# Where softmax sums meet the attended values in the first attention phase: reciprocals turned beside them

## The chip, the cores and the metric

The kernel runs on one core of a Trainium2 chip. The metric is the device time of one execution in microseconds (us). TensorE (PE) multiplies and transposes, VectorE (DVE) and ScalarE (ACT) work elementwise, GpSimd (POOL) does some elementwise work, SyncE (SP) issues the DMAs.

## The reference, cut to what matters

Two layers of cross attention are applied to x of 16 batches x 256 tokens x 512 channels, with 16 heads of 32 channels. Only the first attention matters here:

```python
xq, ctx = layer_norm(x, qn_w, qn_b), layer_norm(context, cn_w, cn_b)
q = (xq @ q_w).reshape(B, N, H, D)
kv = (ctx @ kv_w).reshape(B, M, 2, H, D)
attn = jnp.einsum('bnhd,bmhd->bhnm', q, kv[:, :, 0]) * scale
attn = jnp.where(xa_mask[:, None, :, :], neg, attn)
attn = jax.nn.softmax(attn, axis=-1)
out = jnp.einsum('bhnm,bmhd->bnhd', attn, kv[:, :, 1]).reshape(B, N, C)
x = x + out @ proj_w + proj_b
```

An MLP, a causal self attention and another cross attention with its own MLP follow.

## The kernel before

The program has four phases, one after the other: mask (the attention above), mlp, causal, cross. The mask phase ends at about 722 us of the profiled span of 2908.9 us. Each phase but mlp runs one turn per batch; turns 1 to 14 are a hardware loop. In a turn every engine has its own queue of work, whose order is written out by hand in `mask_turn` (one for each engine), and engines wait for each other through counting semaphores. The turn of batch b also holds the start of batch b+1 (norms, turning to channels, the first queries, keys and values) and the end of batch b-1 (its last heads, the projection).

The 16 heads go in four quarters c of four heads; u counts the heads. For a quarter:

- PE `scores(b, c)` (L1529) makes the scores of four heads in four PSUM banks. It waits for the exponentials of the quarter before.
- DVE `minima` (L1086) adds the mask and takes the minimum of each row, four heads, two instructions a head, with `qk_lo` (L1045) in the middle.
- ACT `exps` (L650) takes the exponentials and leaves the sums of the rows in `sums`, an SBUF tile of 8 values a partition for each quarter (2 halves of the tokens x 4 heads).
- PE `turn_probs` (L1550) transposes them, ACT `copy` (L662) takes them to SBUF, PE `attend` (L1569) multiplies with the values. The quarter's result stands in the first half of the PSUM bank O, as 4 heads x 32 channels on the partitions and 256 tokens along them, and is not yet divided by the sums.
- ACT `attended` (L672) copies it to `OT`; PE `attended` (L1578) turns it to rows of tokens, 2 transposes into the second half of O; DVE `attended` takes the reciprocals of the 8 sums (L1094, tile `rs`) and multiplies (L1100) into `z`.
- For each half p of the channels, PE `post_turn` (L1587) turns z back to channels, 4 transposes into a PSUM bank; ACT `post_hi` (L685) rounds it to the high part of `zT`, DVE `post_lo` (L1150) makes the low part; PE `project` (L160, from `product`) multiplies with the projection matrix, and DVE `project` (L1160) adds it to the residual.

Two stretches of a turn matter below, with PE's order of work. Quarter 0 ends with queries, `post_turn`, keys. After `attend(b, 1)` PE goes on to

```python
                turn_probs(b, 8)
            if nxt:
                scores_taken(b, 10)
                turn_over(b + 1, 2)
                ...
                queries(b + 1, 0)
                scores_taken(b, 11)
                turn_over(b + 1, 3)
```

where `turn_over` (L1477) transposes the next batch's input into score banks that the exponentials must have left. ACT `turned` (L617) scales it, DVE `turned` (L1031, L1033) splits it into a high and a low part, and the next `keys(b + 1, 0, half)` (L160, from cT) wait for these, each half of the product for its own.

Of the kernel before, what the change touches and what calls it, by code (L numbers as in the profile page):

```python
# [13 lines left out]
ALU = mybir.AluOpType  # L14
ACT = mybir.ActivationFunctionType
AX_X = mybir.AxisListType.X

P = 128
# [145 lines left out]
def attention_phase(nc, kind, x_src, ctx_src, mask_src, dst, mats, vecs, common, last):  # L164
# [18 lines left out]
    if masked_ctx:  # L183
        x_in = rest("x_in", [P, TT, C])
        c_in = rest("c_in", [P, TT, C])
        xT = [rest(f"xT_{part}", [P, KC, S], F32R) for part in ("hi", "lo")]
        cT = [rest(f"cT_{part}", [P, KC, S], F32R) for part in ("hi", "lo")]
        QK = rest("qk_parts", [P, 2, 4, S], F32R)
        t32 = rest("t32", [P, 2, 2, S])
        r = room(4 * SLOT, SLOT)  # L190
        prob = r("prob", [P, 4, TT, S])
        V = r("v", [P, TT, H, DH])
        z = r("z", [P, TT, C])
        probT = room(5 * SLOT, SLOT)("probT", [P, 8, 512])
        r = room(6 * SLOT, SLOT)
        zT = [r(f"zT_{part}", [P, KC, S], F32R) for part in ("hi", "lo")]
        res = r("res", [P, TT, C])
        p_bias = r("p_bias", [P, C])
        OT = r("ot", [P, S])
        sums = r("sums", [P, KC, TT, HC])  # L200
        low = r("low", [P, 4, TT])
        rs = r("rs", [P, TT, HC])
        r = room(7 * SLOT, SLOT)
        stage = r("stage", [P, KC, C])
        mask = r("mask", [P, TT, S])
        m_in = r("m_in", [P, TT, S], U8)
        wcol = r("wcol", [P, 4, KC])
        stats = r("stats", [P, 4, 6])
        mv = r("mv", [P, 4, 2])
        minus_mean = r("minus_mean", [P, 4])  # L210
        rstd = r("rstd", [P, 4])
        raw = [probT[:, 0:4, :], probT[:, 4:8, :], prob[:].rearrange("p u t s -> p u (t s)"), stage[:]]
    else:
        xT = [rest(f"xT_{part}", [P, KC, S], F32R) for part in ("hi", "lo")]
        probT = rest("probT", [P, 8, 512])
        prob = rest("prob", [P, 4, TT, S])
        x_in = rest("x_in", [P, TT, C])
        z = rest("z", [P, TT, C])
        res = rest("res", [P, TT, C])
        r = room(3 * SLOT, SLOT)  # L220

        QK = r("qk_parts", [P, 2, 4, S], F32R)
        V = r("v", [P, TT, H, DH])
        OT = r("ot", [P, S])
        sums = r("sums", [P, KC, TT, HC])
        low = r("low", [P, 4, TT])
        rs = r("rs", [P, TT, HC])
        r = room(SLOT, SLOT)
        y = r("y", [P, TT, C])
        Q0 = r("q0", [P, 2, P], F32R)  # L230
        flags = r("flags", [P, S])
        cut = r("cut", [P, 2, S], F32R)
        lens = r("lens", [P, KC])
        nan0 = r("nan0", [P, KC])
        big = r("big", [P, TT])
        m_next = r("m_next", [P, TT])
        m_cur = r("m_cur", [P, TT])
        n_norms = 2 if cross else 1
        minus_mean = [r(f"minus_mean{i}", [P, TT]) for i in range(n_norms)]
        rstd = [r(f"rstd{i}", [P, TT]) for i in range(n_norms)]  # L240
        stats = r("stats", [P, TT, 6])
        mv = r("mv", [P, TT, 2])
# [358 lines left out]
    def scalar(act):  # L601
# [72 lines left out]

        def post_hi(b, p):

            act.wait_ge(s["post_ps"], 2 * (b - 1) + p + 1)
            if cross:

                for i in range(2):  # L680
                    ch = 2 * p + i
                    ins = act.activation(x2T[0][:, ch, :], POST_BANK[p][:, i * S:(i + 1) * S], ACT.Identity,  # L682
                                         scale=gb_col[:, 0, ch:ch + 1])
            else:
                ins = act.activation(zT[0][:, 2 * p:2 * p + 2, :],  # L685
                                     POST_BANK[p][:].rearrange("p (c t) -> p c t", c=2), ACT.Copy)
            ins.then_inc(s["post_hi"], 1)

        def relu(b, p):
# [300 lines left out]
        yield from turn(B, True, False, False)  # L990

    def vector(dve):
        head = {"mask": 7, "causal": 15, "cross": 14}[kind]
        per = {"mask": 6, "causal": 18, "cross": 23}[kind]
        chain = Chain(dve, s["chain"], head, per)
        def matrix_lo(i, quarters=range(KC)):
            for k in quarters:
# [74 lines left out]
        def masks_and_minima(b, u):  # L1072
# [14 lines left out]
                                                   ALU.min, low[:, u % 4, qt:qt + 1])  # L1087
            ins.then_inc(s["masked"], 1)

        def attended(b, c):  # L1090

            dve.wait_ge(s["z_ps"], KC * b + c + 1)
            c = c % KC
            chain.done(dve.reciprocal(rs[:], sums[:, c]))  # L1094
            chain.wait()
            if lengths:

                chain.done(dve.tensor_tensor(rs[:], rs[:], m_cur[:].unsqueeze(2).to_broadcast([P, TT, HC]), ALU.mult))
                chain.wait()
            dve.tensor_tensor(z[:, :, c * P:(c + 1) * P].rearrange("p t (h d) -> p t h d", h=HC),  # L1100
                              Oz, rs[:].unsqueeze(3).to_broadcast([P, TT, HC, DH]), ALU.mult
                              ).then_inc(s["z_done"], 1)
# [37 lines left out]
        def post_lo(b, p):  # L1140
            dve.wait_ge(s["post_hi"], 2 * (b - 1) + p + 1)
            if cross:
                for i in range(2):
                    ch = 2 * p + i
                    ins = dve.scalar_tensor_tensor(out=x2T[1][:, ch, :], in0=POST_BANK[p][:, i * S:(i + 1) * S],  # L1145
                                                   scalar=gb_col[:, 0, ch:ch + 1],
                                                   in1=x2T[0][:, ch, :].bitcast(F32), op0=ALU.mult,
                                                   op1=ALU.subtract)
            else:
                ins = dve.tensor_tensor(zT[1][:, 2 * p:2 * p + 2, :],  # L1150
                                        POST_BANK[p][:].rearrange("p (c t) -> p c t", c=2),
                                        zT[0][:, 2 * p:2 * p + 2, :].bitcast(F32), ALU.subtract)
            ins.then_inc(s["post_lo"], 1)

# [41 lines left out]

        def mask_turn(b, prev, cur, nxt):

            if cur:
                minima(b, 0, (0, 1))  # L1200
                qk_lo(b, 1)
                minima(b, 0, (2, 3))
            if not cur:
                yield ROOM
            if prev:
                attended(b, -1)
            if nxt:
                front(b + 1)
            elif cur:
# [2 lines left out]
                post_lo(b, 1)  # L1212

            if cur:
                minima(b, 1, (0, 1))
                qk_lo(b, 2)
                minima(b, 1, (2, 3))
                if not nxt:
                    yield ROOM
            if prev:  # L1220
                project(b, 0)
            if cur:
                attended(b, 0)
            if nxt:
                turned(b + 1, 0)
                turned(b + 1, 1)

            if cur:
                minima(b, 2, (0, 1))
                qk_lo(b, 3)  # L1230
                minima(b, 2, (2, 3))
# [5 lines left out]
            elif cur:  # L1237
                yield ROOM
            if cur:
                attended(b, 1)  # L1240

            if cur:
                minima(b, 3, (0, 1))
            if nxt:
                qk_lo(b + 1, 0)
# [4 lines left out]
            elif cur:  # L1250
                yield ROOM
            if cur:
                attended(b, 2)
                post_lo(b + 1, 0)
                if not nxt:
                    yield ROOM
# [206 lines left out]
    def tensor(pe):  # L1463
# [110 lines left out]
        def attended(b, c):  # L1574
# [3 lines left out]
                ins = pe.transpose(O[:, S + qt * P:S + (qt + 1) * P], OT[:, qt * P:(qt + 1) * P], ident[:])  # L1578
            ins.then_inc(s["z_ps"], 1)

        def post_turn(b, p):

            src = z if masked_ctx else res
            for i in range(2):
                for t in range(TT):
                    ch = 2 * p + i
# [50 lines left out]
        def mask_turn(b, prev, cur, nxt):  # L1637

            if cur:
                if prev:  # L1640
                    pe.wait_ge(s["post_lo"], 2 * (b - 1) + 1)
                scores(b, 0)
            if prev:
                turn_probs(b, -1)
# [4 lines left out]
            if not cur:  # L1649
                yield ROOM  # L1650
            if prev:
                attend(b, -1)
            if cur:
                values(b, 1, 1)
                turn_probs(b, 0)

            if prev:
                attended(b, -1)
            if cur:
                pe.wait_ge(s["qk_lo"], KC * b + 2)  # L1660
                queries(b, 2, 0)
                turn_probs(b, 1)
                queries(b, 2, 1)

            if prev:
                pe.wait_ge(s["z_done"], KC * b + 1)
                post_turn(b - 1, 1)
            if not cur:
                yield ROOM
            if cur:  # L1670
# [11 lines left out]
                project(b, 0, 0)  # L1682

            if cur:
                attend(b, 0)
            if prev:
                project(b, 0, 1)
# [1 line left out]
                turn_probs(b, 4)  # L1689

            if cur:
                attended(b, 0)
                pe.wait_ge(s["qk_lo"], KC * b + 3)
                queries(b, 3, 0)
                turn_probs(b, 5)
                queries(b, 3, 1)
# [19 lines left out]
                project(b, 1, 0)  # L1716

            if cur:
                attend(b, 1)
            if prev:  # L1720
                project(b, 1, 1)
# [14 lines left out]
            if cur:  # L1736
                turn_probs(b, 9)

            if cur:
                attended(b, 1)  # L1740
            if nxt:
                pe.wait_ge(s["t_lo"], NP * (b + 1) + 3)
                keys(b + 1, 0, 0)
# [17 lines left out]
                values(b + 1, 0, 0)  # L1761

            if cur:
                attend(b, 2)
            if nxt:
                values(b + 1, 0, 1)
            if cur:
                turn_probs(b, 12)

            if cur:  # L1770
                attended(b, 2)
            if nxt:
                pe.wait_ge(s["qk_lo"], KC * (b + 1) + 1)
                queries(b + 1, 1, 0)
# [1 line left out]
                turn_probs(b, 13)  # L1776
            if nxt:
                queries(b + 1, 1, 1)
            if cur:
                pe.wait_ge(s["z_done"], KC * b + 3)  # L1780
                scores_taken(b, 14)
                post_turn(b, 0)

            if nxt:
                keys(b + 1, 1, 0)
# [765 lines left out]
```

## Time and profile before

| | |
|---|---|
| median of 3 runs | 2909.57 us (2909.24 to 2912.53) |
| profiled execution, its time and its span | 2911.72 us, 2908.9 us |
| busy share of the span: PE, PE weight loads | 96%, 84% |
| DVE, ACT, POOL | 60%, 56%, 22% |
| mean granted TensorE clock | 0.985 |

Shares are over all four phases; the mask phase is about a quarter of the span. An instruction's length in the trace overlaps the next one's, so what a piece of work costs an engine is read from start to start.

### The profile page before, as it was taken

The page shows a single profiled execution, that of the slowest core. Times are in us where ns is not written, and L with a number is a line of the kernel's source. Part 1 is how long each engine was busy: PE and PEld are TensorE (multiplying, and loading weights), DVE is VectorE, ACT ScalarE, POOL GpSimd, SP SyncE. Part 2 cuts the span into 40 slices and gives each one's busy share as a digit, 9 for nine tenths or more (in the row PEclk, how much of TensorE's full clock was granted, in tenths as well). Part 3 has the DMA queues.
Part 4 walks back from the last instruction along what each step waited for, and adds up shares of the span by engine and source line. Part 5 has one row for each costly group of instructions (what it writes and reads, how often), then busy time and mean ns, then how long its engine had stood idle before and what let it go on. Part 6 is the DMA issues. An engine that isn't in the chain of part 4 may idle for free. (4 is left out here: it accounts for less than half of the span.)

```text
span 2908.9 us, 69038 instructions
## 1 busy us (share of the span) xinstructions
PE 2800.9 (96%) x24864; PEld 2434.5 (84%) x24864; DVE 1747.2 (60%) x5353; ACT 1634.4 (56%) x4947; POOL 625.4 (22%) x760
## 2 busy tenths in 40 slices
PE   7999999998999999999999999997899999999995
PEld 6888888887788888888889999996788888888884
DVE  5666666666433333333367777776576767777674
ACT  6777777777311111111277777776575666666562
POOL 1111110111000000000013333333132434333243
PEclk9999999999999999999999999998899999999997
DMA  3111111112300000001001111113201111111100
GB/s 115 31 59 59 38 51 59 51 38 77 109 29 29 19 9 29 29 29 65 22 27 59 46 43 43 43 43 106 73 31 44 42 43 43 43 36 36 43 29 22
DMA packets 74804, 134.37 MB, mean 46 GB/s; under 512 B 10096, under 2 KB 10096, under 8 KB 74736
## 3 DMA queue, kind: packets, MB, share of 16 engines
q1 hardware_dynamic: 74736, 133.47, 13.7%
q8 instruction: 42, 0.69, 0.1%
q14 instruction: 26, 0.21, 0.0%
HBM read 99.90 MB, written 33.55 MB: 46 GB/s over the span
## 5 line engine op out<-in xcount | busy, mean ns | idle before, releaser
L2263 ACT ACTIVATE mlp_h<-mlp_f,mlp_b1col 128x512 f32<-128x512 f32 x128 | 88.2, 689 | 548.2 <-PE mlp_f L2406 548.2
L2406 PE MATMUL mlp_f<-mlp_xT_hi,mlp_w 128*128 128x512 f32 x1024 | 336.5, 391 | 5.2 <-PEq L91 5.2
L2334 DVE CAST mlp_hT_hi<-mlp_h 128x512 fp32r<-128x512 f32 x128 | 58.4, 457 | 434.7 <-ACT mlp_h L2263 434.7
L2418 PE MATMUL mlp_acc<-mlp_w,mlp_hT_hi 128*128 128x512 f32 x1024 | 316.9, 391 | 1.0 <-DVE mlp_hT_lo L2336 1.0
L650 ACT ACTIVATE cross_prob<-cross_scores,cross_low 128x256 f32<-128x256 f32 x512 | 237.4, 499 | 14.5 <-DVE cross_low L1080 14.5
L650 ACT ACTIVATE mask_prob<-mask_scores,mask_low 128x256 f32<-128x256 f32 x512 | 236.9, 474 | 11.5 <-DVE mask_low L1086 10.9
L1086 DVE CUSTOM_DVE_ANT_0 mask_scores<-mask_scores,mask_mask 128x256 f32<-128x256 f32 x512 | 201.3, 455 | 62.9 <-PE mask_scores L1529 62.4
L2406 PEld LDWEIGHTS mlp_f<-mlp_xT_hi,mlp_w 128*128 128x128 f32 x1024 | 193.0, 188 | 45.6 <-issue 5.6
L160 PE MATMUL causal_work<-causal_xT_hi,causal_w 128*128 128x256 f32 x1008 | 226.6, 296 | 0.0
L2418 PEld LDWEIGHTS mlp_acc<-mlp_w,mlp_hT_hi 128*128 128x128 f32 x1024 | 191.1, 188 | 40.3 <-DVE mlp_hT_lo L2336 1.4
L650 ACT ACTIVATE causal_prob<-causal_scores,causal_low 128x128 f32<-128x128 f32 (+1 forms) x512 | 211.1, 433 | 21.7 <-DVE causal_low L1086 20.5
L2406 PE MATMUL mlp_f<-mlp_xT_lo,mlp_w 128*128 128x512 f32 x512 | 199.8, 390 | 0.0
L2418 PE MATMUL mlp_acc<-mlp_w,mlp_hT_lo 128*128 128x512 f32 x512 | 199.5, 390 | 0.0
L1086 DVE CUSTOM_DVE_ANT_0 causal_scores<-causal_scores,causal_tri 128x128 f32<-128x128 f32 (+1 forms) x512 | 164.3, 392 | 33.0 <-PE causal_scores L1535 33.0
L160 PEld LDWEIGHTS causal_work<-causal_xT_hi,causal_w 128*128 128x128 f32 x1008 | 169.4, 189 | 12.1 <-issue 12.1
L1080 DVE TENSOR_REDUCE cross_low<-cross_scores 128x2 f32<-128x512 f32 x256 | 159.8, 680 | 14.2 <-PE cross_scores L1535 10.7
L488 POOL TENSOR_SCALAR cross_q<-all_own_head,cross_qk_parts 128x128 fp32r<-128x128 f32 x128 | 59.8, 478 | 421.2 <-DVE cross_qk_parts L1045 411.5
L160 PE MATMUL causal_work<-causal_xT_lo,causal_w 128*128 128x256 f32 x504 | 141.9, 282 | 0.0
L488 POOL TENSOR_SCALAR causal_q<-all_own_head,causal_qk_parts 128x128 fp32r<-128x128 f32 x128 | 57.7, 462 | 389.1 <-DVE causal_qk_parts L1045 381.9
L457 POOL TENSOR_TENSOR mask_rstd<-mask_rstd,all_half 128x4 f32<-128x4 f32 x16 | 16.3, 1019 | 538.8 <-DVE mask_rstd L1017 538.8
L662 ACT ACTIVATE cross_probT<-cross_probsT 128x512 f32<-128x512 f32 x128 | 76.4, 597 | 98.9 <-PE cross_probsT L1550 98.9
L160 PE MATMUL mask_work<-mask_cT_hi,mask_w 128*128 128x256 f32 x504 | 120.8, 303 | 3.8 <-DVE mask_cT_lo L1033 1.5
(276 smaller groups left out, 8275.5 us busy)
## 6 DMA issues: line engine op xcount, KB each, us to landing
mask_x_in<-in_x SPq DMA_DIRECT2D x16, 512.0 KB, 3.7
mask_c_in<-in_ctx SPq DMA_DIRECT2D x16, 512.0 KB, 5.2
mask_res<-in_x SPq DMA_DIRECT2D x16, 512.0 KB, 3.6
after_attention<-mask_res SPq DMA_DIRECT2D x16, 512.0 KB, 5.9
mlp_x<-after_attention SPq DMA_DIRECT2D x8, 1024.0 KB, 5.7
mlp_stage<-in_L_xattn_fc_w SPq DMA_DIRECT2D x8, 1024.0 KB, 5.2
after_layer<-mlp_y SPq DMA_DIRECT2D x8, 1024.0 KB, 4.3
causal_x_in<-after_layer SPq DMA_DIRECT2D x16, 512.0 KB, 4.2
```

What stands on the lines that cost most here:

```text
L160: last = pe.matmul(out, lhs(k, a), rhs(k, c), start=(k == 0 and n == 0), stop=(k == KC - 1 and n == len(PASSES) - 1))
L457: pool.tensor_tensor(rstd[:], rstd[:], common.half[:], ALU.pow).then_inc(s["rstd_ready"], 1)
L488: ins = pool.tensor_scalar(Q0[:, part, :], own_head[:], QK[:, c % 2, 1 - part, 0:1].bitcast(F32), 1.0, ALU.mult, ALU.mult)
L650: ins = act.activation(prob[:, u % 4, qt, 0:w], SC[h][:, FROM[qt]:FROM[qt] + w], ACT.Exp, bias=low[:, u % 4, qt:qt + 1], scale=-1.0, accum ...
L662: act.activation(probT[:, u % 8, 0:n], PT_BANK[u % HC][:, 0:n], ACT.Copy).then_inc(s["copied"], 1)
L1080: ins = dve.tensor_reduce(low[:, u % 4, :], SC[h][:].rearrange("p (t k) -> p t k", t=TT), AX_X, ALU.min)
L1086: ins = dve.tensor_tensor_reduce(SC[h][:, at], SC[h][:, at], extra, 1.0, F32_MAX, ALU.add, ALU.min, low[:, u % 4, qt:qt + 1])
L2263: act.activation(h32[:, m % 2, :], F1[m % 2][:], ACT.Gelu, bias=b1col[:, m:m + 1]).then_inc(s["gelu"], 1)
L2334: dve.tensor_copy(hT[0][:, r, :], h32[:, r, :]).then_inc(s["h_hi"], 1)
L2406: ins = pe.matmul(F1[m % 2][:], W[2 * (m // 4)][:, a, k, m % 4 * P:(m % 4 + 1) * P], xT[p][:, k, :], start=(k == 0 and n == 0), stop=(k == ...
L2418: ins = pe.matmul(ACC[t][:], hT[a][:, m % 2, t * P:(t + 1) * P], W[2 * (m // 4) + 1][:, p, m % 4, :], start=(m == 0 and n == 0), stop=(m = ...
```

## The change

DVE takes the reciprocals with each of the 8 sums repeated over the 32 channels of its head, so that `rs` has 256 values a partition in place of 8 (`over_sums`). It stands at the head of each quarter's minima in DVE's queue. PE turns `rs` into the second half of O right ahead of `attend` (`turn_sums`, 2 transposes), in the place of turning OT. DVE multiplies OT with it (`normed`), channels on the partitions, into `z32`, which `post_hi` and `post_lo` read from SBUF. `post_turn` is gone from the mask phase, and so are the waits around it. The other phases keep their way. The core of the diff:

```diff
-        z = r("z", [P, TT, C])
+        z32 = r("z32", [P, KC, S])
-        rs = r("rs", [P, TT, HC])
+        rs = r("rs", [P, TT, HC, DH])
...
+                act.wait_ge(s["z_done"], KC * (b - 1) + 2 * p + 3)
+                if p == 0 and (not isinstance(b, int) or b > 1):
+                    act.wait_ge(s["proj_ps"], TT * (b - 1))
+                ins = act.activation(zT[0][:, 2 * p:2 * p + 2, :], z32[:, 2 * p:2 * p + 2, :], ACT.Copy)
...
+        def over_sums(b, c):
+            dve.wait_ge(s["exp_done"], UNITS * b + HC * (c + 1))
+            dve.reciprocal(rs[:], sums[:, c % KC].unsqueeze(3).to_broadcast([P, TT, HC, DH])).then_inc(s["rs_done"], 1)
+        def normed(b, c):
+            dve.wait_ge(s["ot_done"], KC * b + c + 1)
+            dve.tensor_tensor(z32[:, c % KC, :], OT[:], O[:, S:2 * S], ALU.mult).then_inc(s["z_done"], 1)
...
             if cur:
+                over_sums(b, 1)
                 minima(b, 2, (0, 1))
                 qk_lo(b, 3)
                 minima(b, 2, (2, 3))
...
+        def turn_sums(b, c):
+            pe.wait_ge(s["rs_done"], KC * b + c + 1)
+            pe.wait_ge(s["z_done"], KC * b + c + 1)
+            for qt in range(TT):
+                pe.transpose(O[:, S + qt * P:S + (qt + 1) * P], rs[:, qt].rearrange("p h d -> p (h d)"), ident[:])
...
             if cur:
-                if prev:
-                    pe.wait_ge(s["post_lo"], 2 * (b - 1) + 1)
                 scores(b, 0)
...
             if prev:
+                turn_sums(b, -1)
                 attend(b, -1)
...
-            if prev:
-                attended(b, -1)
...
-            if prev:
-                pe.wait_ge(s["z_done"], KC * b + 1)
-                post_turn(b - 1, 1)
...
-            if cur:
-                pe.wait_ge(s["z_done"], KC * b + 3)
-                scores_taken(b, 14)
-                post_turn(b, 0)
```

In the same way `over_sums(b, c - 1)` stands ahead of `minima(b, c, ...)` for every quarter, `turn_sums(b, c)` ahead of every `attend(b, c)`, and `normed(b, c)` where DVE's `attended(b, c)` stood. `sums` and `low` move to another place in SBUF.

## Rows read from the trace of the kernel before

**Rows 1.** Windows: each engine's busy us (and instructions), granted TensorE clock, DMA share, GB/s.

```profile
300.00:400.00 100.00, 99.55 (x977) 84.91 (x976) 65.71 (x237) 78.39 (x238) 18.07 (x20) 1.00 0.13 43
```

**Rows 2.** Groups of 60 to 700 us: names, shapes, count; busy us, mean ns; idle before, releaser.

```profile
L160 PEld LDWEIGHTS mask_work<-mask_cT_hi,mask_w 128*128 128x128 f32 x480 | 82.3, 189 | 10.7 <-DVE mask_cT_lo L1033 10.7
...
L1100 DVE TENSOR_TENSOR mask_z<-mask_attended,mask_rs 128x256 f32<-128x256 f32 x60 | 25.5, 424 | 2.1
...
L1587 PE MATMUL mask_attended<-all_ident,mask_z 128*128 128x128 f32 x60 | 9.0, 273 | 0.0
```

**Rows 3.** Timeline of PE, quarter 0: start us, length us, line, output, input, count.

```profile
381.74 0.28 PE L160 MATMUL mask_work<-mask_xT_hi,mask_w 128*128 128x256 f32 x1
381.86 0.60 PE L1587 MATMUL mask_attended<-all_ident,mask_z 128*128 128x128 f32 x4
382.22 0.37 PE L160 MATMUL mask_work<-mask_cT_hi,mask_w 128*128 128x256 f32 x1
382.42 0.28 PE L160 MATMUL mask_work<-mask_cT_lo,mask_w 128*128 128x256 f32 x1
```

**Rows 4.** Timeline of PE, quarters 1 and 2 of the same turn.

```profile
395.00 0.98 PE L1529 MATMUL mask_scores<-mask_qk_parts 32*128 32x256 f32 x24
...
397.89 1.07 PE L1569 MATMUL mask_attended<-mask_probT,mask_v 128*32 128x256 f32 x16
...
400.82 0.60 PE L1477 MATMUL mask_scores<-all_ident,mask_c_in 128*128 128x128 f32 x4
...
404.03 0.39 PE L160 MATMUL mask_work<-mask_cT_hi,mask_w 128*128 128x256 f32 x1
...
405.59 0.39 PE L160 MATMUL mask_work<-mask_cT_hi,mask_w 128*128 128x256 f32 x1
```

**Rows 5.** Timeline of DVE in quarters 1 and 2; the bracket is idle time and its releaser.

```profile
385.44 0.43 DVE L1086 CUSTOM_DVE_ANT_0 mask_scores<-mask_scores,mask_mask 128x256 f32<-128x256 f32 x1 [0.81 <-PE mask_scores L1529]
...
395.47 0.69 DVE L1033 TENSOR_TENSOR mask_xT_lo<-mask_t,mask_xT_hi 128x512 fp32r<-128x512 f32 x1
396.19 0.43 DVE L1086 CUSTOM_DVE_ANT_0 mask_scores<-mask_scores,mask_mask 128x256 f32<-128x256 f32 x1
...
402.82 0.43 DVE L1031 CAST mask_cT_hi<-mask_t 128x512 fp32r<-128x512 f32 x1 [1.55 <-ACT mask_t L617]
...
404.38 0.43 DVE L1031 CAST mask_cT_hi<-mask_t 128x512 fp32r<-128x512 f32 x1 [0.41 <-ACT mask_t L617]
```

**Rows 6.** Timeline of ACT in quarters 1 and 2.

```profile
391.66 0.60 ACT L662 ACTIVATE mask_probT<-mask_scores 128x512 f32<-128x512 f32 x1 [0.53 <-PE mask_scores L1550]
392.89 1.93 ACT L617 ACTIVATE mask_t<-mask_scores,mask_wcol 128x256 f32<-128x256 f32 x4 [0.64 <-PE mask_scores L1477]
...
397.10 0.47 ACT L650 ACTIVATE mask_prob<-mask_scores,mask_low 128x256 f32<-128x256 f32 x1
...
401.26 0.62 ACT L662 ACTIVATE mask_probT<-mask_scores 128x512 f32<-128x512 f32 x1
401.74 1.05 ACT L617 ACTIVATE mask_t<-mask_scores,mask_wcol 128x256 f32<-128x256 f32 x2
403.33 1.02 ACT L617 ACTIVATE mask_t<-mask_scores,mask_wcol 128x256 f32<-128x256 f32 x2 [0.54 <-PE mask_scores L1477]
```

**Rows 7.** Short DVE instructions, from their tile: count, ns min/median/max, first and last start.

```profile
L1094 DVE RECIPROCAL causal_rs<-causal_sums x64: 192/202/206, 1474.3 to 2024.8; 128x8 f32<-128x8 f32 x64
L1098 DVE TENSOR_TENSOR causal_rs<-causal_rs,causal_m_cur x64: 166/167/246, 1474.5 to 2025.1; 128x8 f32<-128x8 f32 x64
...
L1058 DVE RECIPROCAL causal_nan<-causal_lens x64: 149/155/158, 1453.0 to 2006.5; 128x1 f32<-128x1 f32 x64
L1060 DVE TENSOR_SCALAR causal_nan<-causal_nan x64: 152/154/156, 1453.2 to 2006.7; 128x1 f32<-128x1 f32 x64
```

**Rows 8.** Timeline of PE at the end of the mask phase.

```profile
717.39 1.60 PE L1569 MATMUL mask_attended<-mask_probT,mask_v 128*32 128x256 f32 x16
...
721.10 0.47 PE L2406 MATMUL mlp_f<-mlp_xT_hi,mlp_w 128*128 128x512 f32 x1
```

More of the change, by code:

```diff
@@ L199, in attention_phase @@
         OT = r("ot", [P, S])
-        sums = r("sums", [P, KC, TT, HC])
-        low = r("low", [P, 4, TT])
-        rs = r("rs", [P, TT, HC])
+        rs = r("rs", [P, TT, HC, DH])
         r = room(7 * SLOT, SLOT)
@@ L207, in attention_phase @@
         wcol = r("wcol", [P, 4, KC])
+        sums = r("sums", [P, KC, TT, HC])
+        low = r("low", [P, 4, TT])
         stats = r("stats", [P, 4, 6])
@@ L675, in post_hi @@
         def post_hi(b, p):
-            act.wait_ge(s["post_ps"], 2 * (b - 1) + p + 1)
             if cross:
+                act.wait_ge(s["post_ps"], 2 * (b - 1) + p + 1)
                 for i in range(2):
@@ L684, in post_hi @@
             else:
-                ins = act.activation(zT[0][:, 2 * p:2 * p + 2, :],
-                                     POST_BANK[p][:].rearrange("p (c t) -> p c t", c=2), ACT.Copy)
+                act.wait_ge(s["z_done"], KC * (b - 1) + 2 * p + 3)
+                if p == 0 and (not isinstance(b, int) or b > 1):
+                    act.wait_ge(s["proj_ps"], TT * (b - 1))
+                ins = act.activation(zT[0][:, 2 * p:2 * p + 2, :], z32[:, 2 * p:2 * p + 2, :], ACT.Copy)
             ins.then_inc(s["post_hi"], 1)
@@ L992, in vector @@
     def vector(dve):
-        head = {"mask": 7, "causal": 15, "cross": 14}[kind]
-        per = {"mask": 6, "causal": 18, "cross": 23}[kind]
+        head = {"mask": 4, "causal": 15, "cross": 14}[kind]
+        per = {"mask": 2, "causal": 18, "cross": 23}[kind]
         chain = Chain(dve, s["chain"], head, per)
@@ L1095, in attended @@
             chain.wait()
-            if lengths:
-                chain.done(dve.tensor_tensor(rs[:], rs[:], m_cur[:].unsqueeze(2).to_broadcast([P, TT, HC]), ALU.mult))
-                chain.wait()
+            chain.done(dve.tensor_tensor(rs[:], rs[:], m_cur[:].unsqueeze(2).to_broadcast([P, TT, HC]), ALU.mult))
+            chain.wait()
             dve.tensor_tensor(z[:, :, c * P:(c + 1) * P].rearrange("p t (h d) -> p t h d", h=HC),
@@ L1149, in post_lo @@
             else:
-                ins = dve.tensor_tensor(zT[1][:, 2 * p:2 * p + 2, :],
-                                        POST_BANK[p][:].rearrange("p (c t) -> p c t", c=2),
+                ins = dve.tensor_tensor(zT[1][:, 2 * p:2 * p + 2, :], z32[:, 2 * p:2 * p + 2, :],
                                         zT[0][:, 2 * p:2 * p + 2, :].bitcast(F32), ALU.subtract)
@@ L1197, in mask_turn @@
         def mask_turn(b, prev, cur, nxt):
+            if prev:
+                over_sums(b, -1)
             if cur:
@@ L1205, in mask_turn @@
             if prev:
-                attended(b, -1)
+                normed(b, -1)
             if nxt:
@@ L1214, in mask_turn @@
             if cur:
+                over_sums(b, 0)
                 minima(b, 1, (0, 1))
@@ L1222, in mask_turn @@
             if cur:
-                attended(b, 0)
+                normed(b, 0)
             if nxt:
@@ L1239, in mask_turn @@
             if cur:
-                attended(b, 1)
+                normed(b, 1)
             if cur:
+                over_sums(b, 2)
                 minima(b, 3, (0, 1))
@@ L1252, in mask_turn @@
             if cur:
-                attended(b, 2)
+                normed(b, 2)
                 post_lo(b + 1, 0)
@@ L1579, in attended @@
             ins.then_inc(s["z_ps"], 1)
+        def turn_sums(b, c):
[3 more added lines that the diff above has]
+                pe.transpose(O[:, S + qt * P:S + (qt + 1) * P], rs[:, qt].rearrange("p h d -> p (h d)"), ident[:])
         def post_turn(b, p):
-            src = z if masked_ctx else res
+            src = res
             for i in range(2):
@@ L1655, in mask_turn @@
                 turn_probs(b, 0)
-            if prev:
-                attended(b, -1)
             if cur:
@@ L1684, in mask_turn @@
             if cur:
+                turn_sums(b, 0)
                 attend(b, 0)
@@ L1691, in mask_turn @@
             if cur:
-                attended(b, 0)
                 pe.wait_ge(s["qk_lo"], KC * b + 3)
@@ L1718, in mask_turn @@
             if cur:
+                turn_sums(b, 1)
                 attend(b, 1)
@@ L1737, in mask_turn @@
                 turn_probs(b, 9)
-            if cur:
-                attended(b, 1)
             if nxt:
@@ L1763, in mask_turn @@
             if cur:
+                turn_sums(b, 2)
                 attend(b, 2)
@@ L1768, in mask_turn @@
                 turn_probs(b, 12)
-            if cur:
-                attended(b, 2)
             if nxt:
@@ L1778, in mask_turn @@
                 queries(b + 1, 1, 1)
-            if cur:
-                pe.wait_ge(s["z_done"], KC * b + 3)
-                scores_taken(b, 14)
-                post_turn(b, 0)
             if nxt:
```

## Prediction

> **What bounds the kernel now.** I read the windows first: in a hundred microseconds of the mask phase PE is busy for 99.55, at the full granted clock of 1.00, while ACT has 78.39 and DVE 65.71 [rows 1]. So PE's queue sets the pace, and the reader could think that any transpose taken from it is a gain. The groups then show where PE is not its own master: from 60 to 700 us its weight loads sat idle for 10.7 us until DVE had written the low part of cT, and the z that this change is about costs DVE 60 multiplications of 424 ns and PE 60 transposes for each of two banks, of which one is shown [rows 2]. That idle time is small, but it lies in every turn at one place, the keys of the next batch. The timelines of PE, DVE and ACT there show a closed ring [rows 4 to 6]: PE starts `scores(b, 2)` at 395.00; DVE, which ends `turned(b+1, 1)` (its last instruction starts at 395.47), starts the minima at 396.19; ACT starts the exponentials of quarter 2 at 397.10, runs them without a pause worth the name, then `copy(b, 8)` at 401.26 and `turned(b+1, 2)` at 401.74; DVE casts at 402.82; PE starts the first half of the keys at 404.03 and the second at 405.59. In this ring PE waits; elsewhere in the turn it does not. A turn is thus a stretch in which PE sets the time, from the keys round to `turn_over(b+1, 0)`, and the ring of some 10 us, where DVE and ACT set it.
>
> **What PE gains.** A `post_turn` stands between queries and keys. From the last matmul of the queries to the second of the keys is 382.42 - 381.74 = 0.68 us; two plain steps there take 2 x 0.12 (381.86 - 381.74), so the four transposes cost PE 0.44, 0.11 each [rows 3]. Batches have two; 30 of them lie where PE sets the pace (two in each of 15 turns), which gives 30 x 0.44 = 13.2 us. The one of batch 15 ahead of the last turn is beside waits for exponentials and counts nothing. The two transposes of OT become two of rs in each quarter: 0.22 off, 0.22 on, and nothing is summed; they move ahead of `attend`, and if the step between different weight shapes cost another 0.1 us there, 64 of them would be 6 us, a bound that I keep for the range.
>
> At the end of the phase PE waits for OT, turns it, waits for z and turns that: `attend` starts at 717.39 and its 1.60 us end at 718.99, and the mlp's first matmul starts at 721.10 [rows 8]. With only ACT's copy and one multiplication left, both beside that mlp work, PE goes straight on. I take 2.0 of these 2.1 us. Together 15.2 us.
>
> **What DVE pays.** The reciprocal over 256 values is in no row. One value takes 155 ns, where a plain instruction takes 154; eight take 202, where a plain one of the same shape takes 167 [rows 7]. So eight reciprocals cost 35 ns over a plain instruction, 4.4 ns each. A plain one over 256 is 424 ns [rows 2]. That gives 0.424 + 256 x 0.0044 = 1.55 us, which I take, since the fixed part falls out between equal shapes. The floor is the plain 0.42. From one value to eight the medians differ by 47 ns, 6.7 ns a value, so 0.155 + 255 x 0.0067 = 1.87; with the longest of eight and the shortest of one (206 - 149) it is 8.1 ns and 2.22 us, the ceiling.
>
> The Trainium skill bears on this: "VectorE: DVE Perf Modes", in "First, the fixed hardware budget", says that the reciprocal is an iterative divide with a repeat count of 8. Read as eight steps for each value, and with the spacing of the plain rows, it would be near the ceiling and not near the value taken, and it speaks against widening a reciprocal from 8 values to 256. The trace's 35 ns for eight values agree only in that a value costs several plain steps.
>
> The small reciprocal and its wait go (0.2 us a quarter); DVE waits for ACT's OT and not for PE's turn of it, so `normed` comes about 1 us earlier in most quarters. DVE thus has room for four wide reciprocals a turn; what matters is what stands behind each.
>
> - Quarters 3 and 0 of a turn (`over_sums(b, 2)` and `over_sums(b, -1)`): DVE idles before the minima for longer than the instruction takes, or comes free about as `scores` ends. Nothing at 1.55, some tenths at 2.22.
> - Quarter 1 (`over_sums(b, 0)`): DVE idled for 0.81 us before the minima at 385.44 [rows 5]; it also gains about 1 us from the earlier `normed`. The minima come up to 0.3 us late. ACT behind them waits for PE for 0.53 us and again for 0.64 before `turned(b+1, 0)` [rows 6], and swallows 1.17. Cost nothing; without that cover it would be up to 0.3 us a turn.
> - Quarter 2 (`over_sums(b, 1)`): no cover. The instruction can start when the step before gives way, 395.47 + 0.60 = 396.07 (such a 0.69 us instruction is followed after about 0.60), and holds the next for its length less 0.08. The minima start at 396.07 + 1.47 = 397.54 in place of 396.19: 1.35 us late. Queued behind it are the minima, `qk_lo(b, 3)`, DVE's `project(b, 1)` and the turned parts. ACT has no gap up to `turned(b+1, 2)`, so the cast and the first keys are 1.35 late. The second half of the keys follows the first by 1.56 us now, of which about 0.36 is a wait for `turned(b+1, 3)` that then goes, since ACT no longer waits its 0.54 us for PE [rows 4, 6]. PE's turn grows by 1.35 - 0.36 = 0.99 us.
>
> PE also meets two new waits: `turn_sums(b, 1)` needs rs at about 397.6, ahead of an `attend` now at 397.89, so it is just ready; and the step to `turn_over(b+1, 2)`, now 400.82, waits for later exponentials. Both lie inside the 0.99 and are not added. 15 turns have a next batch: 15 x 0.99 = 14.9 us. `post_hi` and `post_lo` work on the same 512 columns from SBUF; they end earlier, not later, since they don't wait for PE, and nobody waits for them.
>
> **The sum.** Against the profiled execution: 2911.7 - 15.2 + 14.9 = 2911.4 us. It stood 2.1 us above the median of the runs, so I predict 2909 us.
>
> **Rivals.** I call no change what lies within 0.2%, about what a measurement of this kernel tells from none: 2903.8 to 2915.4.
>
> 1. The two cancel, as above. Chance 0.48. It holds for a reciprocal of about 1.2 to 2.0 us; own range 2904 to 2915.
> 2. The lateness doesn't bite: the reciprocal is at the floor (0.42 us, minima 0.22 late, less than the 0.36), or the ring has more give than I see. Then 15.2 us are kept: 2894 us. For: PE is busy for 99.55 of 100 us, and its transposes are surely gone. Against: eight reciprocals already take 35 ns too long, and the trace shows DVE as PE's releaser in this ring. It decides below 1.2 us. Halfway, at 0.8 us, it gives 15 x (0.60 - 0.36) = 3.6 us of loss and 2898. Chance 0.29.
> 3. The wide reciprocal is as slow as the ceiling. The minima of quarter 2 are then 2.02 us late and a turn pays 1.66: 15 x 1.66 = 24.9, less 15.2, that is 9.7 us more: 2919 us. It is slower from 2.0 us of reciprocal on. For: 8.1 ns can be read from the extremes, and `over_sums` of quarters 0 and 1 would begin to show (0.3 us a turn is 4 us more, 2923). Against: medians give 4.4 to 6.7. The skill's repeat count in the same section as above, taken at its word, is this case. Chance 0.23.
>
> So faster 0.29, same 0.48, slower 0.23. The two tails beyond 2897 and 2921 hold about a tenth each: the range is 2897 to 2921.
>
> **What would show it.** The reciprocal of 128x256: 1.5 us in case 1, 0.4 in case 2, 2.2 in case 3. DVE's minima of quarter 2 start 1.35 us later after `scores(b, 2)` than the 1.19 us now. PE's group of L1587 has no mask rows left. PE's idle time released by DVE's cT parts or by ACT's exponentials grows from 0.7 to about 1.7 us a turn, in the ring and nowhere else. The mlp's first matmul follows the last `attend` at once. I would be wrong if PE waited for rs in other quarters, if a pair of transposes ahead of `attend` cost more than 0.22 us, or if ACT's chain after the late minima caught up.

## The result and the profile after

The changed kernel takes 2914.39 us (median of 22 runs, 2911.64 to 2919.03) where the kernel before takes 2910.19 (22 runs). The ratio is 1.0014, interval [1.0008, 1.0020]: slower by some 4 us, less than the 0.2% that I had called a difference, but beyond the interval and not the way of the 2909 that I forecast. All ratios here and below compare executions at the usual mean clock of 0.98 or 0.99; one of seven executions of the first experiment's kernel took 3907 us at a mean granted clock of 0.653 and is not in its ratio.

The windows of the profile after, the same stretch as in [rows 1]:

```profile
300.00:400.00 100.00, 97.48 (x959) 82.64 (x958) 76.17 (x230) 77.02 (x233) 17.94 (x18) 1.00 0.14 43
```

PE, which was busy for 99.55, is now at 97.48, at the same clock of 1.00; DVE went from 65.71 to 76.17. PE has less to do and stands idle for more than what it was spared. The waits of 60 to 700 us (who waited for whom: us in total, times, longest) say where:

```profile
PEld mask_work L160 <- DVE mask_cT_lo L1036: 13.7, 14, 1.0
PEld mask_scores L1492 <- issue: 10.5, 14, 0.8
...
PE mask_work L160 <- DVE mask_cT_lo L1036: 10.4, 14, 0.7
...
PE mask_scores L1492 <- ACT mask_prob L650: 7.3, 14, 0.5
...
PEld mask_attended L1601 <- DVE mask_rs L1096: 4.8, 14, 0.4
```

PE waits once a turn for the low part of cT, once for the exponentials to leave the score banks (L1492 is `turn_over`), and shortly for rs. All three lie in the ring. The weight loads' rows (PEld) add up to (13.7 + 10.5 + 4.8) / 14 = 2.1 us a turn, where the kernel before had the 10.7 us of [rows 2], 0.8 a turn; I had expected 0.7 to become 1.7. PE's timeline there, the turn that answers to [rows 4]:

```profile
394.75 0.98 PE L1544 MATMUL mask_scores<-mask_qk_parts 32*128 32x256 f32 x24
...
397.62 0.44 PE L1601 MATMUL mask_attended<-all_ident,mask_rs 128*128 128x128 f32 x2
397.99 1.07 PE L1584 MATMUL mask_attended<-mask_probT,mask_v 128*32 128x256 f32 x16
...
401.60 0.65 PE L1492 MATMUL mask_scores<-all_ident,mask_c_in 128*128 128x128 f32 x4 [0.52 <-ACT mask_prob L650]
...
405.30 0.38 PE L160 MATMUL mask_work<-mask_cT_hi,mask_w 128*128 128x256 f32 x1 [0.74 <-DVE mask_cT_lo L1036]
...
407.35 0.98 PE L1544 MATMUL mask_scores<-mask_qk_parts 32*128 32x256 f32 x24
```

From the scores of quarter 2 to those of quarter 3 PE takes 407.35 - 394.75 = 12.60 us. In the kernel before the first of these start at 395.00 [rows 4] and the second, in the same timeline, here:

```profile
406.49 0.98 PE L1529 MATMUL mask_scores<-mask_qk_parts 32*128 32x256 f32 x24
```

That is 11.49, so the ring grew by 1.11 us. A whole turn (from a quarter 0 to the next) went from 42.98 to 43.22 us, so the rest of it shrank by 0.87. DVE and ACT in the ring, answering to [rows 5, 6]:

```profile
395.21 0.69 DVE L1036 TENSOR_TENSOR mask_xT_lo<-mask_t,mask_xT_hi 128x512 fp32r<-128x512 f32 x1
395.82 1.75 DVE L1096 RECIPROCAL mask_rs<-mask_sums 128x256 f32<-128x256 f32 x1
397.48 0.41 DVE L1089 CUSTOM_DVE_ANT_0 mask_scores<-mask_scores,mask_mask 128x256 f32<-128x256 f32 x1
```

```profile
396.35 0.60 ACT L662 ACTIVATE mask_probT<-mask_probsT 128x512 f32<-128x512 f32 x1 [0.81 <-PE mask_probsT L1565]
398.37 0.47 ACT L650 ACTIVATE mask_prob<-mask_scores,mask_low 128x256 f32<-128x256 f32 x1 [1.42 <-DVE mask_low L1089]
```

The minima start 2.73 us after the scores of their quarter (397.48 - 394.75), 1.19 before: 1.54 late. ACT, which had no gap, waits 1.42 us for them. The instruction in between is the term that I had to guess; its tile's rows give all 64 (ns min/median/max):

```profile
L1096 DVE RECIPROCAL mask_rs<-mask_sums x64: 1735/1746/1749, 39.1 to 718.8; 128x256 f32<-128x256 f32 x64
```

1.746 us, where I took 1.55. At the end of the phase the last `attend` is at once followed by the mlp, as forecast, but PE had stood 1.43 us for rs in the last turn, which answers to [rows 8]:

```profile
709.56 0.44 PE L1601 MATMUL mask_attended<-all_ident,mask_rs 128*128 128x128 f32 x2 [1.43 <-DVE mask_rs L1096]
...
721.06 1.07 PE L1584 MATMUL mask_attended<-mask_probT,mask_v 128*32 128x256 f32 x16
722.06 0.50 PE L2416 MATMUL mlp_f<-mlp_xT_hi,mlp_w 128*128 128x512 f32 x1
```

### The profile page after: what moved, and what is told of

Its sections match the earlier page's. It is cut to its first block and busy times, and to the rows that moved or that the text cites. A ratio compares the mean times of both kernels' runs of the same rounds, so it can differ in the third digit from the quotient of the medians.

```text
span 2911.2 us, 68814 instructions
## 1 busy us (share of the span) xinstructions
PE 2789.9 (96%) x24736; PEld 2419.3 (83%) x24736; DVE 1834.4 (63%) x5353; ACT 1637.6 (56%) x4947; POOL 632.9 (22%) x760
## 5 line engine op out<-in xcount | busy, mean ns | idle before, releaser
L650 ACT ACTIVATE cross_prob<-cross_scores,cross_low 128x256 f32<-128x256 f32 x512 | 237.8, 500 | 12.8 <-DVE cross_low L1083 12.7
L1083 DVE TENSOR_REDUCE cross_low<-cross_scores 128x2 f32<-128x512 f32 x256 | 159.8, 680 | 13.6 <-PE cross_scores L1550 10.2
L662 ACT ACTIVATE mask_probT<-mask_probsT 128x512 f32<-128x512 f32 x128 | 76.9, 601 | 93.9 <-PE mask_probsT L1565 93.9
```

Of the source, the lines that this page charges most:

```text
L650: ins = act.activation(prob[:, u % 4, qt, 0:w], SC[h][:, FROM[qt]:FROM[qt] + w], ACT.Exp, bias=low[:, u % 4, qt:qt + 1], scale=-1.0, accum ...
L662: act.activation(probT[:, u % 8, 0:n], PT_BANK[u % HC][:, 0:n], ACT.Copy).then_inc(s["copied"], 1)
L1083: ins = dve.tensor_reduce(low[:, u % 4, :], SC[h][:].rearrange("p (t k) -> p t k", t=TT), AX_X, ALU.min)
```

## The experiments

Theory A: the wide reciprocal ahead of quarter 2's minima lengthens the ring, and only that costs. Theory B: PE's wait for rs costs. Theory C: the added work on DVE costs wherever it stands. Each change below is made to the changed kernel unless said otherwise; "turn" is read from the starts of the scores of one quarter in two turns. Ratios are to the kernel before, run beside each on the same chip (2910.53 to 2911.91 us there); the changed kernel was not run again beside them, and the kernel before alone stood up to 1.7 us higher there than beside it, so a difference to its 2914.39 us is good to about 2 us.

**The same work, earlier in the queue**

```diff
                 normed(b, 0)
+                over_sums(b, 1)
             if nxt:
                 turned(b + 1, 0)
                 turned(b + 1, 1)
             if cur:
-                over_sums(b, 1)
                 minima(b, 2, (0, 1))
```

> The changed kernel with one move: quarter 1's over_sums stands right behind normed(b, 0), ahead of turned(b+1, 0), where VectorE idles, and no longer ahead of quarter 2's minima. Nothing is added or left out. Theory A (the 1.75 us reciprocal ahead of quarter 2's minima makes the ring longer by 1.11 us a turn, and nothing else costs): quarter 2 to quarter 3 scores go back from 12.60 to about 11.5 us, 15 turns give 16.7 us back: about 2898 us, ratio to before 0.996. Theory B (the cost is TensorE's wait for rs ahead of attend, 0.34 us a turn): at most 5 us back, about 2909 us. Theory C (VectorE's added work as such, wherever it stands): no change, about 2914 us.

Measured: 2901.72 us, ratio 0.9966 [0.9955, 0.9978]. The turn is 42.36 us (366.46 to 408.82), the ring 11.71 (387.16 to 398.87). DVE's timeline shows the instruction where DVE idled for ACT:

```profile
383.61 0.41 DVE L1101 TENSOR_TENSOR mask_z<-mask_ot,mask_attended 128x256 f32<-128x256 f32 x1
383.94 1.75 DVE L1096 RECIPROCAL mask_rs<-mask_sums 128x256 f32<-128x256 f32 x1
386.10 0.43 DVE L1034 CAST mask_xT_hi<-mask_t 128x512 fp32r<-128x512 f32 x1 [0.41 <-ACT mask_t L617]
...
388.34 0.43 DVE L1089 CUSTOM_DVE_ANT_0 mask_scores<-mask_scores,mask_mask 128x256 f32<-128x256 f32 x1
```

It is as long as before, DVE waits 0.41 us after it all the same, and the minima start 1.18 us after their scores (387.16). C is out: no work was taken from DVE. B alone would have given 5 us, and 13 came. That is 3 to 4 us short of A's 16.7; the ring is 11.71 and not 11.5, and where these 0.2 us a turn come from is told in the account of the prediction.

**The same place, a short instruction**

```diff
+            if c == 1:
+                dve.tensor_copy(rs[:], sums[:, c % KC].unsqueeze(3).to_broadcast([P, TT, HC, DH])).then_inc(s["rs_done"], 1)
+                return
```

> The changed kernel with quarter 1's wide reciprocal as a plain copy of the same shape (so this quarter's division is left out: the values are multiplied by the sums). Theory A: the instruction takes 0.42 in place of 1.75 us, the minima of quarter 2 are about 0.2 us late, which the slack ahead of the second half of the keys hides: about 2898 us, as with the move. Theory B: TensorE no longer waits for rs, at most 5 us back, 2909 us. Theory C: VectorE has 1.3 us less a turn of some 7 us added: 3 us back at most, 2911 us.

Measured: 2899.07 us, 0.9958 [0.9945, 0.9971]; a turn of 42.31 us. Taking the long instruction out of this place and making it short in this place come to the same, as A says.

**One wide reciprocal more, in two places**

```diff
             dve.reciprocal(rs[:], ...).then_inc(s["rs_done"], 1)
+            if c == 1:
+                dve.reciprocal(spare[:], sums[:, c % KC].unsqueeze(3).to_broadcast([P, TT, HC, DH]))
```

The second kernel has `c == 0` in this line.

> The changed kernel with quarter 1's wide reciprocal made a second time into an unused tile, behind the first, so that rs itself is not later. Theory A: the minima of quarter 2 start another 1.67 us late with no cover, 15 x 1.67 = 25 us more: about 2939 us, ratio 1.010. Theory B: rs is as early as before, no change: 2914 us. Theory C: the same extra work costs the same wherever it stands, so this run and the one with the second reciprocal in quarter 1 come out alike.

Measured: 2944.68 us, 1.0118 [1.0104, 1.0133]: 1.04% or 30 us above the changed kernel, 25 expected. The turn read at 400 us is 44.83; 14 turns take 629.92 us in place of 605.24, which is 24.7: twelve of them are 1.6 us longer, as expected, and two are 2.7 longer, which stays unexplained. The other 5 or so come in turn 0 and in the last turn. That disproves B as the cause: rs was not later.

> The changed kernel with quarter 0's wide reciprocal (ahead of quarter 1's minima) made a second time into an unused tile, behind the first. Theory A: the minima of quarter 1 start 1.7 us late; ScalarE's slack behind them (0.37 and 0.62 us in the profile after) swallows 1.0, the other 0.7 a turn reaches the turned parts of the next batch: 15 x 0.7 = 10 us more, about 2924 us, clearly less than the same work in quarter 2. Theory B: no change, 2914 us. Theory C: like the run with it in quarter 2.

Measured: 2920.76 us, 1.0036 [1.0023, 1.0048]: 0.22% or 6 us above the changed kernel, where 10 were expected, and a fifth of the same work in quarter 2. The turn is 43.60, 0.38 longer, against 1.6 to 1.8 there. So some 1.3 of the 1.67 us were swallowed and not 1.0; turn 0, though, is 3.5 us longer, as it is with the second reciprocal in quarter 2. C falls again.

**The cost without the gain**: the kernel before, with one wide reciprocal into a dead tile ahead of quarter 2's minima.

```diff
             if cur:
+                dve.wait_ge(s["exp_done"], UNITS * b + HC * 2)
+                dve.reciprocal(spare[:], sums[:, 1].unsqueeze(3).to_broadcast([P, TT, HC, DH]))
                 minima(b, 2, (0, 1))
```

> The kernel before with one instruction more: a wide reciprocal (128x256, as in the change) into an unused tile, ahead of quarter 2's minima. None of the change's gain is in it. Theory A: minima 1.75 - 0.20 = 1.55 us late, less the 0.36 that the second half of the keys waits anyway: 1.19 us a turn, 15 turns give 18 us: about 2929 us, ratio 1.006. Theory B (TensorE's wait for rs): there is no such wait here, no change, 2911 us. Theory C (work on VectorE in general): the four wide reciprocals together would cost what the whole change lost, so one costs about 4 us: 2915 us.

Measured: 2935.07 us, 1.0081 [1.0067, 1.0095]: 24 us, 18 expected. The turns show what was expected: 14 of them take 617.59 us in place of 601.88, 1.12 each, where 1.19 was worked out. Turn 0 adds 2.6 and the last turn 2.1, so that the phase from its first scores is 20.5 us longer; as these start 1.5 us earlier in this profile, the mlp's first matmul starts 18.9 us later (740.0 against 721.1). About 5 us more come in the later phases, which the edit does not touch; in the profiled execution about 3 of them are the clock's, told in the last section.

**The gain without the cost**: the 8 reciprocals, then a plain copy that spreads them.

```diff
-            dve.reciprocal(rs[:], sums[:, c % KC].unsqueeze(3).to_broadcast([P, TT, HC, DH])).then_inc(s["rs_done"], 1)
+            dve.reciprocal(rs8[:], sums[:, c % KC]).then_inc(s["rs8_done"], 1)
+            dve.wait_ge(s["rs8_done"], KC * b + c + 1)
+            dve.tensor_copy(rs[:], rs8[:].unsqueeze(3).to_broadcast([P, TT, HC, DH])).then_inc(s["rs_done"], 1)
```

> The changed kernel, each wide reciprocal made as one over the 8 sums and a plain copy that repeats each over 32 channels; same places in the queue. 0.20 + 0.03 + 0.42 = 0.65 us in place of 1.75. Theory A: minima of quarter 2 are 0.46 us late, of which 0.36 is hidden: 0.1 us a turn is left of 1.1: about 2899 us, ratio 0.996. Theory C: VectorE has 4.4 us less a turn, so the same direction: this run tells the size of the instruction as the term, not the place.

Measured: 2898.49 us, 0.9957 [0.9944, 0.9971], the 2899 expected; a turn of 42.31 us.

> Both: the small reciprocal with the plain copy, and quarter 1's of them moved behind normed(b, 0). Theory A: the ring is as in the kernel before and the two post_turns are saved, and nothing is left to win from the move once the instruction is short: within 3 us of the run without the move, about 2898 us. It is the version that should beat both kernels.

Measured: 2895.95 us, 0.9952 [0.9938, 0.9966]. The same kernel once more, beside the last two below:

> The version with the small reciprocal and the early spread once more, beside the two others on one chip: 2896 us, ratio 0.995; 13 us below the one with the dead transposes and 17 below the one with the wide reciprocal in quarter 2 by Theory A.

Measured: 2897.78, 0.9958 [0.9944, 0.9971]. It beats both kernels: 13 to 15 us under the kernel before, some 17 under the changed one. Reciprocal and spread in its first profile, one of each of the 64:

```profile
384.08 0.20 DVE L1097 RECIPROCAL mask_rs<-mask_sums 128x8 f32<-128x8 f32 x1
384.31 0.29 DVE L1099 COPY mask_rs<-mask_rs 128x256 f32<-128x256 f32 x1
```

The two take 0.52 us from start to end, a third of the wide one.

**The new places of sums and low**, in the kernel before, nothing else.

```diff
-        sums = r("sums", [P, KC, TT, HC])
-        low = r("low", [P, 4, TT])
         rs = r("rs", [P, TT, HC])
         r = room(7 * SLOT, SLOT)
...
         wcol = r("wcol", [P, 4, KC])
+        sums = r("sums", [P, KC, TT, HC])
+        low = r("low", [P, 4, TT])
```

> The kernel before with sums and low at their new places in SBUF and nothing else. Every theory but that of the places in SBUF: no change, 2911 us. If the new places cost something, up to the 4 us of the change would show here.

Measured: 2911.63 us, 1.0004 [0.9995, 1.0013]. The interval alone would leave room for up to 3.8 us, but the profile doesn't: the turn is 42.98 us, as before, and the phase from its first scores 688.46 in place of 688.27.

**The transposes put back.** To the version with the small and early reciprocal:

```diff
+        def dead_turn():
+            for i in range(2):
+                for t in range(TT):
+                    pe.transpose(SC[2][:, i * S + t * P:i * S + (t + 1) * P], own_head[:], ident[:])
...
                 queries(b, 2, 1)
+            if prev and cur:
+                scores_taken(b, 2)
+                dead_turn()
...
                 queries(b + 1, 1, 1)
+            if nxt:
+                scores_taken(b, 14)
+                dead_turn()
```

> The version with the small reciprocal and the early spread, with four transposes of a constant tile put back at each of the two places where post_turn stood (they write a free score bank, nobody reads them, and only the wait for the bank's exponentials is kept). Theory A: the gain of the change is these transposes and nothing else, 0.44 us each time, 29 times: 13 us more than the version without them, about 2909 us, ratio 0.9995, which is the kernel before but for the end of the phase. Rival D (the gain is in the waits of post_turn and of the turned OT, or in VectorE's earlier normed): clearly less than 13 us come back, 2900 us or so.

Measured: 2910.51 us, 0.9999 [0.9990, 1.0008], 12.7 us above the version without them on the same chip. The turn is 43.20 us, 0.86 longer, for two times four transposes (they stand in the program 30 times, not 29). So the gain in the turns is these transposes, and rival D, with 2900 us, is out.

**The wide reciprocal in quarter 2 alone**, the small one with the spread in the other three (in `over_sums`: `if c == 1` the wide one, else the small one).

> The changed kernel with the small reciprocal and the plain spread in three quarters and the wide reciprocal left only ahead of quarter 2's minima. Theory A: only this one sets the time, so the turn stays at 43.2 us; the last turn, where the wide one of another quarter kept TensorE waiting, may win 1 to 2 us: about 2913 us, ratio 1.001. Theory C (VectorE's work as such): three of four parts of the added work are gone, so three quarters of the way from 2914 to 2898 are made: 2902 us.

Measured: 2912.84 us, 1.0008 [0.9999, 1.0017]; a turn of 43.2 us, as in the changed kernel (43.22). Three quarters of DVE's added work gone brought less than 2 us. One instruction in one place costs 15 us against the version with none wide on the same chip, which also has quarter 1's pair moved; that move was worth at most 3 us once the pair was short (2898.49 against 2895.95).

## Why the prediction was wrong

**What bounds the kernel: right outside the ring, half right inside.** Doubling the reciprocal in the ring cost four to five times as much as in quarter 1, so what delays the minima there counts. But in the kernel before, the wait that ends last in the ring goes back to PE itself. ACT idled 0.54 us for `turn_over(b+1, 3)` [rows 6], which PE's timeline shows here:

```profile
402.69 0.60 PE L1477 MATMUL mask_scores<-all_ident,mask_c_in 128*128 128x128 f32 x4
```

PE works without a pause from the scores of quarter 2 up to this, 7.69 us, and the second half of the keys follows 2.90 us later (405.59), through ACT and DVE. That is why the first 0.36 us of lateness were free, and why more work for PE ahead of that point is not.

**PE's gain of 0.44 us for each `post_turn`: right.** The part of the turn outside the ring shrank by 0.87 (0.88 worked out), and transposes put back cost 0.86.

**The reciprocal: the step that failed, a mis-sized term that turned the sign.** I wrote that the fixed part "falls out between equal shapes" and took 4.4 ns a value from one comparison at 8 values; 256 values take 1.746 us. From 8 values (0.200) it is (1746 - 200) / 248 = 6.2 ns a value, and from 1 value to 8 the rows had said 6.7 [rows 7]. The slope of one instruction over its own lengths was the better ground: the prediction's own 1.87 us from it, put into the same sum, gives 2914 us, a hit that is luck in part, since 1.87 is too long. 0.2 us too little, 15 times, is 2.9 us.

**The lateness and its price: right.** With 1.746 in my formula the minima come 1.55 late (1.54 measured) and PE pays 1.19 (1.11 measured). The wait of the second half of the keys hid its 0.36 and a little more: 15 x 0.08 = 1.2 us to the good.

**"0.22 off, 0.22 on, and nothing is summed": wrong in the ring.** There the pair moved from behind `turn_over(b+1, 3)`, where PE waited for cT afterwards, to ahead of `attend(b, 1)`. The version with the short reciprocal, moved early, shows it:

```profile
387.24 0.98 PE L1547 MATMUL mask_scores<-mask_qk_parts 32*128 32x256 f32 x24
...
393.26 0.60 PE L1495 MATMUL mask_scores<-all_ident,mask_c_in 128*128 128x128 f32 x4
...
395.13 0.60 PE L1495 MATMUL mask_scores<-all_ident,mask_c_in 128*128 128x128 f32 x4
...
398.04 0.39 PE L160 MATMUL mask_work<-mask_cT_hi,mask_w 128*128 128x256 f32 x1 [0.35 <-DVE mask_cT_lo L1037]
```

Its `turn_over(b+1, 2)` starts 6.02 us after the scores of quarter 2, 5.82 before [rows 4], `turn_over(b+1, 3)` 7.89 in place of 7.69, the keys again 2.91 later, and the ring is 11.70 in place of 11.49. That is 0.2 us a turn, 3 us in all, which even the best version pays. In the changed kernel the late exponentials cover it.

**The end: half right.** I took 2.0 us there and 0.44 for the last turn's `post_turn`. The step from the last `attend` to the mlp fell from 3.71 us to 1.00 [rows 8], but from quarter 0 of the last turn (674.82 before, 676.76 after) to the mlp's start the phase is only 46.28 - 45.30 = 0.98 us shorter. So 1.5 us of the forecast 2.44 is missing. In this turn wide reciprocals stand ahead of the minima of quarters 2 and 3 while the mlp's opening work is also in DVE's queue: the step from the scores of quarter 2 to those of quarter 3 grew from 9.28 to 9.97 us, and PE stood 1.43 us for rs in quarter 3, which the prediction had named as a sign of being wrong. With the short reciprocal in the same places the time from quarter 0 to the mlp is 43.90 us, 2.38 less than before, nearly the whole forecast.

Together: forecast for the mask phase from its first scores -0.3 us; reciprocal +2.9, ring -1.2, end +1.5 makes +2.9. Ring and end all but cancel, so the reciprocal alone carries the sign. Measured in the profiles: from the first scores (32.83 and 31.05) to the mlp (721.10 and 722.06) 688.27 and 691.01, so +2.7. The medians' +4.2, interval 2.3 to 5.8, takes that in; where the other 1.5 us come from, or whether they are noise, stays open.

**The rivals.** 1.746 us lies in the band of rival 1 (1.2 to 2.0), and 2914.39 in its own range: the two sides nearly cancel, but not as evenly as in my sum. The give in the ring of rival 2 was not there beyond the 0.4 us that I had counted. Rival 3 had the right sign and its mechanism, but not its price of 2.2 us; the repeat count of 8 that the Trainium skill names ("VectorE: DVE Perf Modes", "First, the fixed hardware budget") is not eight spacings a value here: 6.2 ns measured, beside 1.04 for a plain instruction (a subtraction of 512 values takes 691 ns, the multiplication of 256 takes 424 [rows 2]; the difference over 256).

## What to carry to other kernels

An instruction is priced by what stands behind it in its queue: the same 1.75 us cost nothing measurable beside idle time 4 us earlier and over 1 us a turn at the head of the chain. When a slow operation works on repeated values, do it on the few and spread the results with a copy. And size an operation that the trace doesn't show from its own slope over lengths; where such a size decides the sign, measure it first.

## What the runs showed of the hardware

A copy from SBUF to SBUF of 128x256 f32, repeating each value 32 times, took 293 ns, not the 424 of the multiplication of that shape [rows 2] that I had taken as a plain price and put into two of the expectations. The Trainium skill ("Vector Engine (DVE) Microarchitecture Reference", "5.1 Performance modes — why throughput varies by op and dtype") states a mode of two results a cycle for copies between SBUF tiles and none such for two f32 tensors; the trace agrees, since 293 less a fixed 157 (424 - 256 x 1.04) is half a plain spacing a value.

The granted clock has dips where one phase hands over to the next, and their length can differ for the same work. The windows of the kernel before and then of the one with a dead reciprocal, causal to cross; the second kernel is some 20 us later here, so that the rows answer to each other:

```profile
2070.00:2080.00 10.00, 6.03 (x49) 4.77 (x47) 5.81 (x13) 6.38 (x17) 0.00 (x0) 0.83 0.24 87
2080.00:2090.00 10.00, 10.00 (x88) 8.73 (x89) 3.35 (x8) 3.43 (x13) 0.00 (x0) 0.66 0.52 177
2090.00:2100.00 10.00, 7.68 (x86) 7.07 (x86) 5.58 (x15) 6.39 (x17) 1.44 (x4) 1.00 0.01 2
```

```profile
2090.00:2100.00 10.00, 6.04 (x41) 4.01 (x39) 5.90 (x13) 7.09 (x20) 0.00 (x0) 0.69 0.14 44
2100.00:2110.00 10.00, 10.00 (x74) 9.67 (x70) 0.86 (x4) 1.07 (x2) 0.00 (x0) 0.50 0.35 101
2110.00:2120.00 10.00, 8.34 (x78) 7.15 (x75) 5.08 (x14) 8.14 (x25) 0.72 (x2) 0.95 0.31 121
```

1.00 is the level of 2.4 GHz and 0.50 that of 1.2; values between are stretches with both. In both kernels the clock falls in a window in which PE was busy for only 6.0 of 10 us. In the first it is low for 10 us in all, in the second for 17. The same holds over all 13 profiles of this case: in ten the clock is low for 10.2 us here and the time from the cross phase's first matmul to the end is 900.5 to 901.9 us; in the other three (dead reciprocal; wide reciprocal early; short reciprocal in place) it is low for 17.1 us, and that time is 904.7 to 904.9. So the longer dip goes with some 3 us; the 6.9 us more at half the clock can cost no more than 3.4. What decides between the two, and whether a kernel keeps to one of them in its executions without a profile, stays open. For a forecast within 0.2% it is an error that no sum over one phase holds.
